# An LSTM recurrence of four interleaved chains: two VectorE steps of each slot are issued earlier

## The reference

```python
def step(carry, xt):
    h, c = carry
    zg = xt @ Wi + h @ Wh + b
    i, f, g, o = jnp.split(zg, 4, axis=-1)
    c = jax.nn.sigmoid(f) * c + jax.nn.sigmoid(i) * jnp.tanh(g)
    h = jax.nn.sigmoid(o) * jnp.tanh(c)
    return ((h, c), h)
_, hs = lax.scan(step, (h0, h0), jnp.swapaxes(x, 0, 1))
```

## Time and profile before

| what | value |
| --- | --- |
| three runs: lowest, median, highest | 5639.88, 5642.22, 5645.06 us |
| profiled execution, its own time | 5641.04 us |
| span of its trace | 5639.1 us |
| mean granted TensorE clock over the span | 0.975 |
| TensorE (matmul) busy | 5230.6 us, 93% of the span |
| VectorE busy | 4163.9 us, 74% |
| ScalarE busy | 2326.0 us, 41% |
| GpSimd busy | 1144.1 us, 20% |
| first and last transpose of the recurrence | 2244.8 and 5077.9 us |

### The profile page before, as it was taken

The page is one execution under the profiler, slowest core; times in us unless marked ns, Lnnn a source line. Parts: engine busy times, 40 slices in busy tenths (PEclk is TensorE's granted clock), DMA queues, the critical chain, the costliest instruction groups (busy, mean ns, idle before and its releaser), DMA issues. The chain is left out here.

```text
span 5639.1 us, 260566 instructions
## 1 busy us (share of the span) xinstructions
PE 5230.6 (93%) x108704; PEld 3565.2 (63%) x108704; DVE 4163.9 (74%) x19277; ACT 2326.0 (41%) x8421; POOL 1144.1 (20%) x5133
## 2 busy tenths in 40 slices
PE   7888879999999996999999999999999999998895
PEld 4445533333333332888888888888888888884442
DVE  4555566666666665999999999999999999991224
ACT  2333356555555553333333333333333333332332
POOL 0000001111111110333333333333333333330000
PEclk9998989999999998999999999999999999999997
DMA  0003354445444533011111111011110111102110
GB/s 13 0 0 108 117 125 83 98 98 103 93 95 102 106 77 150 16 37 22 37 27 25 37 22 37 22 30 37 23 37 21 31 37 23 37 0 84 68 37 12
DMA packets 378077, 300.18 MB, mean 53 GB/s; under 512 B 145993, under 2 KB 357065, under 8 KB 372458
## 3 DMA queue, kind: packets, MB, share of 16 engines
q1 hardware_dynamic: 377886, 298.01, 22.2%
HBM read 178.94 MB, written 119.01 MB: 53 GB/s over the span
## 5 line engine op out<-in xcount | busy, mean ns | idle before, releaser
L1386 PE MATMUL bank<-lparts,lstate 128*32 128x256 bf16 x98304 | 2781.0, 273 | 101.6 <-DVE lstate L1432 54.9
L1386 PEld LDWEIGHTS bank<-lparts,lstate 128*32 128x32 bf16 x98304 | 2450.2, 97 | 432.9 <-DVE lstate L1432 250.9
L1463 ACT ACTIVATE ltc<-lgc 128x16 f32<-128x16 f32 x2049 | 442.5, 216 | 1758.5 <-DVE lgc L1418 1758.2
L1397 DVE STREAM_TRANSPOSE ltz<-bank 128x256 f32<-128x256 f32 x2048 | 921.7, 450 | 92.2 <-PE bank L1386 18.9
L1479 POOL TENSOR_TENSOR wh<-lgate,ltc 128x16 f32<-128x16 f32 x2052 | 465.4, 227 | 1934.5 <-ACT ltc L1463 1861.0
L1114 DVE TENSOR_REDUCE bnegmax<-bank 128x1 f32<-128x512 f32 x1024 | 655.1, 684 | 221.3 <-PE bank L972 221.0
L1202 ACT ACTIVATE wh<-bank 128x512 f32<-128x512 f32 x1024 | 554.6, 600 | 370.6 <-PE bank L990 370.1
L1486 POOL COPY ltz<-wh 128x64 f32<-128x64 f32 x2048 | 603.2, 295 | 0.0
L1404 DVE TENSOR_TENSOR lhalf<-ltz 128x128 f32<-128x128 f32 x2048 | 577.7, 282 | 11.0 <-POOL ltz L1486 10.7
L1414 DVE TENSOR_TENSOR lprod<-lgate,lgc 128x32 f32<-128x32 f32 x2049 | 478.6, 234 | 45.6 <-ACT lgc L1459 45.6
L1052 PE MATMUL bank<-xT,bw 128*128 128x512 f32 x1024 | 487.3, 600 | 17.0 <-DVE bzs L1135 16.2
(11 more groups left out here) (211 smaller groups left out, 4719.3 us busy)
## 6 DMA issues: line engine op xcount, KB each, us to landing
zx<-bzs SPq DMA_DIRECT2D x32, 2048.0 KB, 7.3
wh<-zx SPq DMA_DIRECT2D x64, 1024.0 KB, 7.4
qk<-eparts SPq DMA_DIRECT2D x96, 256.0 KB, 2.6
bqp<-qk SPq DMA_DIRECT2D x192, 128.0 KB, 4.9
bkp<-qk SPq DMA_DIRECT2D x192, 128.0 KB, 7.9
hs<-wh SPq DMA_DIRECT2D x32, 512.0 KB, 5.8
cmemT<-hs SPq DMA_DIRECT2D x32, 512.0 KB, 4.3
vx<-evx SPq DMA_DIRECT2D x16, 544.0 KB, 3.7
```

The lines of the kernel that those rows point to most:

```text
L1386: last = nc.tensor.matmul(bank[x][32 * q:32 * q + 32, 0:256], top[:, x, e, k].rearrange("p m r -> p (m r)"), parts[:, way, g, k, n, e, q], ...
L1397: nc.vector.transpose(tz[:, x].rearrange("p (n w) -> p n w", w=SLOT)[:, :, 0:32], bank[x][:, 0:256].rearrange("p (n c) -> p n c", n=BLOCKS ...
L1463: nc.scalar.activation(tc[:, x], gc[:, x, 1], ACT.Tanh).then_inc(tanhed[x], 1)
```

## The change

In every slot VectorE now issues the new state of n-2 ahead of the block transpose of n (it stood behind it), and the cell of n-1 ahead of the pair sums of n (it stood behind them and behind the last part of the state). The arithmetic and its operands are untouched, and no wait, buffer or semaphore is changed. Behind the loop two instructions of the drain change places once.

```diff
                             x2, t2 = (x - 2) % chains, first + (i + (x - 2) // chains)
+                            new_state(x2, t2)
                             turn_products(x, first + i)
-                            new_state(x2, t2)
                             multiply(x1, t1)
                             rest_of_state(x2, t2)
+                            cell(x1, t1)
                             sum_pairs(x, first + i)
                             last_of_state(x2, t2)
-                            cell(x1, t1)
                             sum_halves(x, first + i)
+                new_state(2, S - 1)
                 multiply(3, S - 1)
-                new_state(2, S - 1)
                 cell(3, S - 1)
                 new_state(3, S - 1)
```

## The result

The changed kernel takes 5554.83 us (median of 4 runs, 5550.52 to 5559.09), the kernel before 5641.05 in the same comparison: a ratio of 0.9845, 95% interval 0.9833 to 0.9858, or 86 us. The forecast was 5584 us with a range of 5557 to 5630. The direction and the loop were right.

What follows compares the result with a forecast made beforehand. The bound was a two-slot loop through VectorE and TensorE, pace (T + 1.77) / 2; T from 0.93 to 0.87 gives 1.32 us a slot against 1.35, 61 us, less disturbances 58: 5642 - 58 = 5584 us, range 5557 to 5630.

Steps and rivals of the forecast that it cites:

- The loop and its formula: Two-slot loop from VectorE's finished state through TensorE to the transpose two slots later; pace (T + 1.77) / 2.
- T: Time from the transpose's start to the start of L1432, last part of the state, same slot; 0.93 us before.
- Step 1: New state issued ahead of the transpose leaves T; behind the transpose it costs 0.05 us.
- Step 2: Cell ahead of the pair sums enters T with 0.09 us; new T taken as 0.87, ends 0.85 and 0.88.
- Step 3: GpSimd's COPY, starting at 1.26 us, lies under the transpose alone and stops holding VectorE; 0.10 us of T goes.
- Step 4: Slot's end: new state starts at 1.19 at the latest, transpose possible at 1.28, due at 1.32; cover 0.04 us.
- The rival at 1.40 a slot: GpSimd's product waits for the half sums, then holds the new state; slot 1.39 to 1.40, 5744 us; chance 0.11.
- Step 5: Gates ready at 0.27 to 0.30 us of the slot, ahead of the multiply at 0.37; no new wait.
- The sum: 1.32 us a slot against 1.35, 0.03 x 2048 = 61 us, becoming 58 because slots at table loads gain nothing.
- TensorE becomes the bound: If T is 0.85 or less, TensorE's 1.31 us a slot sets the pace: 82 us gained, 5560 us; chance 0.17.
- the idle 0.17: TensorE's idle time per pair of slots, 0.17 to 0.18 us, ended by VectorE's last part of the state.

## Why the prediction was wrong, point by point

**The loop and its formula**: right. T fell from 0.93 to 0.85, and with T stretched to 1.11 the formula gave 1.44 a slot where 1.455 came out. With T at 1.02 it gave 1.395 and about 1.40 came out, but there the way over the gates gives the same.

**Step 1, the new state leaves the loop**: right, and it costs nothing ahead of the transpose, but only because the cell moved with it; alone it made the kernel 1.2% slower.

**Step 2, the new T**: this step failed. Forecast 0.87, with 0.12 from multiply to rest, read from a slot in which the multiply was the second instruction behind the transpose. Directly behind it, the multiply took 0.15 instead of 0.18 and the rest followed after 0.07 (3502.17 to 3502.24). From there to the cell were 0.12, not 0.10, the others as forecast: 0.37 + 0.07 + 0.12 + 0.09 + 0.20 = 0.85. I named 0.85 as an end and gave it to the rival.

**Step 3, the collision goes**: right. It was forecast for 1.26 of the slot, and the COPY starts at 1.23. Its price, 0.10 of T, was if anything low: pushed back, the COPY cost 0.17.

**Step 4, the cover**: the new state started 1.11 behind the transpose, not 1.19, and took 0.20 beside GpSimd's product. The transpose was due at the very end of it and not late. The product holds it by 0.03 us (0.20 against 0.17). The rival at 1.40 a slot did not come, because the product did not wait for the half sums: it started at 3502.86, inside them, and took its 0.23 all the same. The prediction argued against that rival from a new state that took 0.13 beside the product; that row could not carry it, as one directly behind the transpose takes 0.13 with or without GpSimd.

**Step 5, the gates**: right in kind, the multiply starts at 0.37 and waits for nothing.

**The sum**: 0.03 x 2048 should have been 0.04 x 2048 = 82 us, which is the rival *TensorE becomes the bound*. It got 0.17, and it is what happened: 81 us in the recurrence. The chance was too low: I took 0.87 for settled, though my own readings of T went from 0.85 to 0.88, and forecast and rival lay only 0.01 us of a slot apart. The rival's last sentence, that without the idle 0.17 TensorE could do 1.265, was wrong too: without any break it takes 1.31 (41.88 us for 32), and the two chains behind a break take 2.52 and not 2.62. Its room before was (2.70 - 2.62)/2 = 0.04 a slot, where the added matmuls found 0.05.

**The range**: it ended at 5557, 3 us under the rival's 5560. Of the measured 86 us the recurrence explains 81. The other 5 are no effect of the change, as far as the profiles show: the stages in front of the recurrence scatter by 8 us, and the range left no room for that.

## What to carry to other kernels

In a software pipeline on engines that execute in order, find the closed loop first, write it as a sum of start-to-start times, and ask of each instruction whether it stands in the loop; here the loop spans two slots, so moving an instruction out pays half of its time, until the next resource is full. Check the chains that the move makes longer as well: here each half of the edit was worthless or harmful alone, and the six other orders of the same eight instructions that ran came out between no change and 3.5% slower than the order before. When two bounds come out within 1% of each other, as 1.32 and 1.31 did here, don't give one of them most of the chance, and test the floor by adding work that nobody waits for.

## What the runs showed of the hardware that was not expected

- Which instruction stands directly behind a 0.45 us transpose changes its price: a multiply took 0.15 there and let the next start after 0.07, one place later 0.18 and 0.12. Where it had to wait for the gates in that same place, it took 0.19 and the next started after 0.10.
- Lengthening the body of ScalarE's loop from 16 to 32 steps added 2.4 us of idle time per turn, and behind it TensorE, idle for 3.98 us, ran at a granted clock of 0.50. That made the kernel 34 us slower though it halved the table loads.
- A one-column Sigmoid in front of the first Tanh halves the table loads of a turn, 1.28 us each.
